# First scan of a four-layer kernel: the low halves of the projection weights computed by GpSimd instead of VectorE

## The reference

```python
x = x + L0(x, cond)    # attention, 16 heads of 16
x = x + L1(cond, cond, x, coupling, bias)          # scan over 128 time steps
x = x + L2(x, cond, ...)    # modulated attention, 16 heads of 128, and a feed-forward part
x = x + L3(cond, x, ...)    # GRU, scan over 128 time steps

# L1, the first scan: one step
def derivative(q, p, drive):
    dq = q - q**3 / 3.0 - p + drive + tanh(q) @ coupling.T + bias
    dp = EPSILON * (q + ALPHA - BETA * p)
    return dq, dp
# four derivatives (Runge-Kutta), the second to fourth at states made from the one before;
# then q and p are advanced and clipped
```

## Time and profile before

| | us |
|---|---|
| median of 3 runs | 1674.68 |
| the 3 runs | 1674.72, 1669.46, 1674.68 |
| the profiled execution | 1674.92 |
| its span, first to last instruction | 1673.2 |
| the first scan in it, steps 0 to 127 | 226.1 to 890.2 |
| steps 6 to 29 of it, which hold the low pieces | 256.05 to 383.25 |

### The profile page before, as it was taken

The page is one execution under the profiler, slowest core; times in us unless marked ns, Lnnn a source line. Parts: engine busy times, 40 slices in busy tenths (PEclk is TensorE's granted clock), DMA queues, the critical chain, the costliest instruction groups (busy, mean ns, idle before and its releaser), DMA issues. The chain is left out here.

```text
span 1673.2 us, 47650 instructions
## 1 busy us (share of the span) xinstructions
PE 1382.7 (83%) x16714; PEld 1069.0 (64%) x16714; DVE 1220.5 (73%) x6967; ACT 837.1 (50%) x3144; POOL 314.5 (19%) x616
## 2 busy tenths in 40 slices
PE   6989984445599959995998978989896699999865
PEld 4468753334466646664667867888883477777755
DVE  3368779999999999999995235666664557666754
ACT  5669833332455555554553226666654544444322
POOL 2026601111211121112111012222221211111110
PEclk8989975555599969995999989999998798979755
DMA  2000020100023203320335688676711300000000
GB/s 96 0 1 3 2 89 27 52 27 2 2 96 109 90 14 103 109 90 8 107 111 189 193 254 242 195 214 174 214 26 51 89 2 3 3 15 3 15 16 15
DMA packets 102839, 127.65 MB, mean 76 GB/s; under 512 B 6108, under 2 KB 79432, under 8 KB 97352
## 3 DMA queue, kind: packets, MB, share of 16 engines
q1 hardware_dynamic: 101744, 122.20, 23.8%
q0 software_dynamic: 272, 2.10, 0.6%
q10 hardware_dynamic: 584, 0.31, 0.1%
HBM read 70.06 MB, written 54.53 MB: 74 GB/s over the span
## 5 line engine op out<-in xcount | busy, mean ns | idle before, releaser
L1020 PE MATMUL bank<-s_tanh_hi,coup_hi 128*128 128x16 f16 x2048 | 136.6, 176 | 151.6 <-ACT s_tanh_hi L1010 150.3
L1020 PEld LDWEIGHTS bank<-s_tanh_hi,coup_hi 128*128 128x128 f16 x2048 | 91.4, 102 | 253.3 <-ACT s_tanh_hi L1010 248.8
L918 POOL TENSOR_SCALAR s_p_scaled<-s_p 128x32 f32<-128x32 f32 x128 | 37.4, 292 | 570.3 <-DVE s_p L901 550.6
L1010 ACT ACTIVATE s_tanh_hi<-s_s 128x32 f16<-128x32 f32 x256 | 58.8, 230 | 161.7 <-DVE s_s L835 158.4
L1532 ACT ACTIVATE prob<-bank,neg_max 128x128 f32<-128x128 f32 x256 | 90.5, 366 | 95.3 <-DVE neg_max L1572 95.3
L1020 PE MATMUL bank<-s_tanh_lo,coup_hi 128*128 128x16 f16 x2048 | 135.8, 176 | 2.3
L1020 PE MATMUL bank<-s_tanh_hi,coup_lo 128*128 128x16 f16 x2048 | 127.3, 171 | 0.0
L664 PE MATMUL bank<-x_hi,w_hi 128*128 128x512 f32 x256 | 120.3, 470 | 0.0
L1596 DVE TENSOR_TENSOR o_lo<-bank,o_hi 128x512 fp32r<-128x512 f32 x64 | 44.2, 691 | 91.5 <-ACT o_hi L1543 91.5
L1020 PEld LDWEIGHTS bank<-s_tanh_lo,coup_hi 128*128 128x128 f16 x2048 | 88.9, 101 | 31.6 <-DVE s_tanh_lo L829 1.1
L1818 PE MATMUL bank<-h_hi,w_h_hi 128*128 128x16 f16 x1536 | 91.4, 172 | 21.3 <-DVE h_hi L2038 21.1
(11 more groups left out here) (312 smaller groups left out, 4444.2 us busy)
## 6 DMA issues: line engine op xcount, KB each, us to landing
queries<-tile_stage SPq DMA_DIRECT2D x64, 256.0 KB, 2.3
keys<-tile_stage SPq DMA_DIRECT2D x64, 256.0 KB, 2.3
values<-tile_stage SPq DMA_DIRECT2D x64, 256.0 KB, 2.4
v<-values SPq DMA_DIRECT2D x64, 256.0 KB, 6.0
q_raw<-queries SPq DMA_DIRECT2D x10, 1024.0 KB, 9.9
k<-keys SPq DMA_DIRECT2D x10, 1024.0 KB, 12.1
x<-in_L_cond_qkv_w_dram SPq DMA_DIRECT2D x6, 1024.0 KB, 5.6
x<-queries SPq DMA_DIRECT2D x6, 1024.0 KB, 9.8
```

The source lines that it names most:

```text
L918: G.tensor_scalar(p_scaled, p, P_IN_P, None, MUL).then_inc(pool_done, 1)
L1010: A.activation(th_hi[:, :], s, ACT.Tanh, scale=scale).then_inc(hi_ready, 1)
L1020: ins = nc.tensor.matmul(coupled[:, B * m:B * m + B], w[:, o:o + P], th[:, B * c:B * c + B], start=(first and c == 0 and m == 0), stop=(la ...
```

## The change

`w_low` is taken out of DVE's pieces. POOL computes the same 96 subtractions, with the same operands, results and semaphore: four in each of the steps 6 to 29, behind its two operations of the step, with a wait for the high part (`wh_ready`) ahead of each four.

```diff
+W_STEP = 6
@@ scan1, vector
-            def w_low(k):
-                m, o = k // 16, 128 * (k % 16)
-                part, c = divmod(m, C)
-                if k % 4 == 0:
-                    dve.wait_ge(wh_ready, k // 4 + 1)
-                V.tensor_tensor(g.w2_l[:, part, c, o:o + 128], w_raw[:, c, o:o + 128], g.w2_h[:, part, c, o:o + 128].bitcast(F32),
-                                SUB).then_inc(wl_ready, 1)
-
@@ scan1, vector, piece(i)
-                if W_AT + 4 <= i < W_AT + 100:
-                    w_low(i - W_AT - 4)
@@ scan1, gpsimd
                 G.tensor_scalar(p_scaled, p, P_IN_P, None, MUL).then_inc(pool_done, 1)
                 G.tensor_scalar(g3, drive[:, W1 * j:W1 * j + W1], 1.0 / 3, None, MUL).then_inc(pool_done, 1)
+                if W_STEP <= j < W_STEP + 24:
+                    for k in range(4 * (j - W_STEP), 4 * (j - W_STEP) + 4):
+                        m, o = k // 16, 128 * (k % 16)
+                        part, c = divmod(m, C)
+                        if k % 4 == 0:
+                            pool.wait_ge(wh_ready, k // 4 + 1)
+                        G.tensor_tensor(g.w2_l[:, part, c, o:o + 128], w_raw[:, c, o:o + 128],
+                                        g.w2_h[:, part, c, o:o + 128].bitcast(F32), SUB).then_inc(wl_ready, 1)
```

## The result

The changed kernel takes 1689.44 us (median of 3 runs, 1686.95 to 1689.85) against 1674.68: a recorded ratio of 1.0095 (that of the two medians is 1.0088), 95% interval 1.0069 to 1.0120. The profiled execution has a span of 1688.1 us, 14.9 above the one before.

What follows compares the result with a forecast made beforehand. DVE was taken as the full engine in steps 6 to 29. Removal saves 0.35 us a step, port holds add 0.62, POOL's own time nothing: +0.27 over 24 steps, +6.5 us, about 1681.2; range 1668 to 1690.

Steps and rivals of the forecast that it cites:

- What bounds the stretch: Scan steps 6 to 29: DVE is the full engine, busy for all of the 126.00 us.
- what removal is worth: Taking 96 operations off DVE in steps 6 to 29 saves 0.35 us a step, at most 8.4 us.
- The pieces' own time: POOL's four subtractions a step, 0.43 us each, fit its spare time and add nothing.
- The mechanism: In the scan, DVE operations with two SBUF inputs wait while POOL's reading of SBUF holds the shared port.
- The hold: Each POOL piece in the scan holds the port for 0.25 us: 128 columns at 1.66 ns, plus 0.04.
- What passes between two holds: First two rounds of a step: some DVE operations run between POOL's holds; losses are 0.24, 0.23, 0.06 and 0.20 us.
- The hand timeline: One scan step worked: first two rounds take 3.12 instead of 2.50 us, +0.62; step 5.57 against 5.30.
- The third: Scan pieces hold the port for whole 0.43 us records, passing one DVE operation each; +15 us, 1690; chance 0.13.
- The first rival: Holds falling into DVE's port gaps around line 835 cost nothing; price 0, 1671.5 to 1678 us; chance 0.20.
- The second: No port trouble with small scan tiles, holds below about 0.08 us; gains 6.5 to 8.4 us, 1667; chance 0.12.

Runs made afterwards that it cites:

- x1_memset: Changed kernel with POOL's 96 pieces writing zeros instead of subtracting; 1662.66 us against 1671.30 for the kernel before, ratio 0.9950.
- x2: Changed kernel with POOL's pieces multiplying one 128-column tile by 1 instead of subtracting two; 1662.06 us in a single run.
- x4: Changed kernel with one POOL piece in each round, started when DVE has done the round's `rest`; 1673.48 us against 1671.30 for the kernel before, ratio 1.0015.
- x8: The changed kernel once more, unaltered, beside the kernel before on another chip; 1690.87 us against 1670.01, ratio 1.0120.
- x5: Changed kernel with POOL subtracting 32 of each 128 columns and filling the rest with zeros; 1661.85 us in a single run.

## Why the prediction was right in sign and wrong in size

- **What bounds the stretch, and what removal is worth: right.** 8.4 us, measured 8.6 by the medians and 7.4 by the steps (x1_memset), where the instructions' own time is 27 us.
- **The pieces' own time: right.** 0.41 us each in a row against 0.43; POOL idle for 3.78 us before each `p_scaled`; no wait for high parts or reloads shows.
- **The mechanism: right.** The earlier trace rows showed it, x1 and x2 confirm it: what holds DVE's two-input operations is POOL's reading. Line 826 (one input in PSUM) is not held even within a piece's reading (x4). For line 833 (a single input) nothing is shown, since no piece was reading while it ran.
- **The hold: mis-sized, the term that failed.** I took 0.25 us from 1.66 ns a column plus 0.04. It measured 0.28 behind the first piece and 0.31 in a row. The 1.66 came from an operation whose second input is a small tile repeated along the columns; two full tiles cost 2.1. Four holds at 0.31 instead of 0.25 are at most 0.24 us a step.
- **What passes between two holds: the larger failure.** The hand timeline let two or three DVE operations through between holds and gave the held ones 0.24, 0.23, 0.06 and 0.20 us of loss. In the trace exactly one passes, since each waits its turn behind the next piece, and all four pieces cost the full 0.29 to 0.31. The pieces also began at 0.68 us of the step, not 0.77, and stretched the first round so that none fell into the second, where I had counted on room. Four times 0.3 is 1.2, less almost no room: +1.17 in the first round instead of +0.42 and +0.20 in two. The step is 4.95 + 1.16 = 6.11 instead of 5.57: over 24 steps, 24 x 0.54 = 13 us more than forecast. The medians show 8.3 of it in the first comparison (14.8 - 6.5) and 14.4 in x8 (20.9 - 6.5).
- **The rivals.** The third had the lockstep, one DVE operation to a piece, and its 1690 is near the 1689.4. In part that is luck: it added 0.6 us a step and the steps took 0.81 more, and only the high median of before made the two agree. Its reason, that the whole record holds, is refuted by x2 for a piece with one input, and a two-input piece of 0.45 us lets go 0.31 us after its start; and it subtracted gaps of 0.25 us that were not there. The first rival (holds that fall into the gaps are free) is true as a mechanism, as x4 shows, but back-to-back pieces do not fall there by themselves. The second needed holds under 0.08 us: that is the 32-column piece of x5, not this one.

## What to carry over

Moving small work from DVE to POOL beside a chain of DVE operations with two SBUF inputs charges the chain for POOL's reads, not for POOL's time, and this chain, with 0.1 us between its operations, paid for back-to-back pieces almost in full. Start such a piece by a semaphore so that it reads while DVE works from PSUM or waits, and see that POOL's own duties to the chain do not come late for it. And a lane's slack is not a budget: before spreading a cost over two rounds, ask whether the first of them simply grows until it holds all of it.

## What the runs showed of the hardware

- POOL's hold on DVE's two-input operations follows what POOL reads: two inputs of 32, 128 and 512 columns held line 820 for 0.07, 0.28 and 1.08 us (records of 0.25, 0.45 and 1.26); with one input of 128 columns, pieces every 0.53 us held an operation that began 0.12 us behind one for 0.10; a write of 128 columns held none.
- A POOL operation on 128 columns with one input and a constant (0.53 us in a row) is slower than one with two inputs (0.41), and yet disturbs less.
- A held DVE instruction counts as busy: 142.73 us in steps 6 to 29, where 127.20 were counted with the 96 pieces still on DVE.
- The stretch between the scans, the same work in every version, took 458.3 to 468.3 us from one profiled execution to another, at a granted clock of 0.82 or 0.78 in its last 77 us.
